# Two neighbouring scans of 1024 elements as one of 2048, with a zero factor where the second begins

## The reference

```python
x = x + 0.5 * ffn(layernorm(x), W1, b1, W2, b2)
x = x + ssm(layernorm(x), ...)
x = x + 0.5 * ffn(layernorm(x), W1, b1, W2, b2)
```

```python
u  = silu(conv4(x_in) + conv_b); dt = softplus(x_in[:, :32] @ Wdt.T + bdt); A = -exp(A_log)
h  = h * exp(dt * A) + dt * Bm * u      # for each channel and state, token by token, h = 0 first
y  = sum over states of h * Cm;  out = (y * silu(z)) @ Wo.T + bo + x * mean(Dv)
```

## Time and profile before

| | |
|---|---|
| runs shown | 768.38, 767.89, 770.54 us, median 768.38 |
| profiled execution | 768.11 us, span 766.3 us |
| VectorE busy | 669.7 us (87%) |
| TensorE busy | 640.7 us (84%), mean granted clock 0.919 |
| ScalarE busy | 603.2 us (79%) |
| GpSimd busy | 301.7 us (39%) |

### The profile page before, as it was taken

The page is one execution under the profiler, slowest core; times in us unless marked ns, Lnnn a source line. Parts: engine busy times, 40 slices in busy tenths (PEclk is TensorE's granted clock), DMA queues, the critical chain, the costliest instruction groups (busy, mean ns, idle before and its releaser), DMA issues. The chain is left out here.

```text
span 766.3 us, 8284 instructions
## 1 busy us (share of the span) xinstructions
PE 640.7 (84%) x2912; PEld 331.8 (43%) x2912; DVE 669.7 (87%) x463; ACT 603.2 (79%) x1066; POOL 301.7 (39%) x189
## 2 busy tenths in 40 slices
PE   7967786889886999979898999967867997874958
PEld 5642333364342466445244574622322654241727
DVE  2436948779999999999999999999999999999791
ACT  2478896779798989998788989898889787946454
POOL 0107020034344598569920767066940060600030
PEclk9997898989997899999999999996988999896979
DMA  8330476350838070421567150705161504205001
GB/s 299 139 137 28 160 219 184 125 178 28 313 117 313 1 246 2 172 103 60 215 198 269 50 198 13 262 1 219 28 216 59 216 31 176 99 28 219 2 0 56
DMA packets 40026, 103.08 MB, mean 135 GB/s; under 512 B 4080, under 2 KB 13040, under 8 KB 39984
## 3 DMA queue, kind: packets, MB, share of 16 engines
q1 hardware_dynamic: 37424, 94.40, 33.7%
q10 hardware_dynamic: 2560, 8.14, 4.5%
HBM read 23.08 MB, written 4.19 MB: 36 GB/s over the span
## 5 line engine op out<-in xcount | busy, mean ns | idle before, releaser
L1089 ACT ACTIVATE G<-RD,COL 128x1024 f32<-128x1024 f32 (+1 forms) x288 | 280.0, 1043 | 62.0 <-PE Y L1376 55.6
L1209 DVE TENSOR_TENSOR_SCAN G<-G,STT,RV 128x1024 f32<-128x1024 f32 (+1 forms) x160 | 312.5, 2015 | 6.4 <-ACT G L1089 6.4
L1209 DVE TENSOR_TENSOR_SCAN G<-G,RV 128x1024 f32<-128x1024 f32 (+1 forms) x128 | 268.9, 2157 | 13.4 <-ACT G L1089 13.4
L1376 PE MATMUL Y<-G,RW 128*32 128x512 f32 x1024 | 143.7, 678 | 62.2 <-DVE G L1209 58.9
L823 POOL TENSOR_SCALAR LV<-LV 128x4 f32<-128x4 f32 x19 | 16.2, 854 | 298.0 <-ACT XN L910 297.7
L1376 PEld LDWEIGHTS Y<-G,RW 128*32 128x32 f32 x1024 | 27.8, 116 | 143.2 <-DVE G L1209 81.5
L849 POOL TENSOR_SCALAR XN<-X,LV 128x256 f32<-128x256 f32 x38 | 83.9, 2212 | 2.0
L1343 PE MATMUL MB<-XI,DIAG 128*64 128x512 f32 x248 | 62.8, 644 | 13.0 <-DMA XI<-XI 11.1
L1302 PE MATMUL MB<-MT,XF 128*128 128x256 f32 x240 | 62.3, 406 | 13.3 <-ACT MT L952 7.6
L832 POOL TENSOR_TENSOR LV<-LV,HALF 128x4 f32<-128x4 f32 (+1 forms) x25 | 45.9, 1837 | 63.5 <-DVE LV L1164 61.9
L1321 PE MATMUL MB<-XT,WI 128*128 128x512 f32 x128 | 64.1, 629 | 3.7 <-ACT XT L936 3.7
(11 more groups left out here) (93 smaller groups left out, 774.5 us busy)
## 6 DMA issues: line engine op xcount, KB each, us to landing
RD<-DW SPq DMA_DIRECT2D x60, 512.0 KB, 3.8
RV<-DW SPq DMA_DIRECT2D x60, 512.0 KB, 4.7
W<-in_w SPq DMA_DIRECT2D x48, 256.5 KB, 3.7
XI<-XI ACTq DMA_DIRECT2D x30, 256.5 KB, 5.0
X<-in_x SPq DMA_DIRECT2D x8, 512.0 KB, 5.6
out<-X SPq DMA_DIRECT2D x7, 512.0 KB, 3.2
G<-in_w SPq DMA_DIRECT2D x4, 513.0 KB, 7.8
RV<-in_w SPq DMA_DIRECT2D x4, 513.0 KB, 12.3
```

The costliest lines, as they stand in the source:

```text
L1089: eng.activation(G[:, i % NG, t0:t1], RD[:, q, t0:t1], ACT.Exp, scale=NAC[:, states(i):states(i) + 1]).then_inc(sems["exp"])
L1209: eng.tensor_tensor_scan(g, g, RV[:, (4 * k + q) % NR, t0:t1], STT[:, idx:idx + 1] if goes_on else 0.0, ALU.mult, ALU.add).then_inc(sems[" ...
L1376: ins = eng.matmul(Y[32 * q:32 * q + 32, 512 * h:512 * h + 512], RW[:, states(i + o), :], G[:, (i + o) % NG, 512 * h:512 * h + 512], start ...
```

## The change

In blocks 1, 2, 3, 8, 9, 10 and 11 (`paired`), scan q even and scan q + 1 become one instruction over 2048 elements: their G tiles and their RV tiles are neighbours. So that the second half begins with state zero, its first factor is made zero: the first column of RD[:, 1] and RD[:, 3] holds 1e30, and exp(1e30 * NAC) is 0, with NAC at most -1e-20. The copies into RD[:, 1] and RD[:, 3] leave out the first column in parts 0 and 2 (1023 elements a row in place of 1024). ScalarE writes the column twice in the program: at the start, and after the exp of 7/15 since part 1 overwrites it. The instruction waits for the exp and the RV copy of both scans, and it raises the semaphore by 2.

```diff
+def paired(i):
+    k = UNITS[i][0]
+    return runs(k) == 1 and k // 4 % 2 == 0
...
+                if n == AT[7, 0, 15]:
+                    do("huge", 1)
...
+                    if k // 4 % 2 == 0 and q % 2 and t0 == 0:
+                        t0 = 1
                     eng.dma_start(RD[:, q, t0:t1], fourfold(DW[q:P:4, 0, t0:t1])
...
+                elif stage == "huge":
+                    n, = a
+                    e.wait_ge("half")
+                    if n:
+                        e.wait_ge("exp", AT[7, 0, 15])
+                    eng.activation(RD[:, 1:4:2, 0], START[:, :], ACT.Copy).then_inc(sems["huge"])
...
-                    eng.tensor_scalar(NAC, NAC, -1.0, None, ALU.mult).then_inc(sems["nac"])
+                    eng.tensor_scalar(NAC, NAC, -1.0, -LEAST, ALU.mult, ALU.min).then_inc(sems["nac"])
...
-                    g = G[:, i % NG, t0:t1]
-                    eng.tensor_tensor_scan(g, g, RV[:, (4 * k + q) % NR, t0:t1], STT[:, idx:idx + 1] if goes_on else 0.0,
-                                           ALU.mult, ALU.add).then_inc(sems["scan"])
+                    if paired(i):
+                        if q % 2 == 0:
+                            e.wait_ge("repw", k, q + 1, 0)
+                            e.wait_ge("exp", i + 1)
+                            g = G[:, i % NG:i % NG + 2, :].rearrange("p a n -> p (a n)")
+                            r = (4 * k + q) % NR
+                            eng.tensor_tensor_scan(g, g, RV[:, r:r + 2, :].rearrange("p a n -> p (a n)"), 0.0,
+                                                   ALU.mult, ALU.add).then_inc(sems["scan"], 2)
+                    else:
+                        ...
```

More of the change, by code:

```diff
@@ L14 @@
 EPS = 1e-5
+HUGE, LEAST = 1e30, 1e-20
 TOP = 17.0
@@ L513, in schedule @@
         do(stage)
+    do("huge", 0)
     a, b, c = norm(0), norm(1), norm(2)
@@ L660, in build @@
         ZERO = sb("ZERO", [P, 3])
+        START = sb("START", [P, 2])
         TOPC = sb("TOPC", [P, 4])
@@ L817, in do @@
                     eng.memset(ZERO[:, :], 0.0)
+                    eng.memset(START[:, :], HUGE)
                     eng.memset(HALF[:, :], -0.5).then_inc(sems["half"])
@@ L1081, in do @@
                     e.wait_ge("nac")
+                    e.wait_ge("huge", k // 8)
                     e.wait_ge("mm", 7)
@@ L1207, in do @@
                         e.wait_ge("save", AT[ko, po, 4 * m])
-                    g = G[:, i % NG, t0:t1]
-                    eng.tensor_tensor_scan(g, g, RV[:, (4 * k + q) % NR, t0:t1], STT[:, idx:idx + 1] if goes_on else 0.0,
-                                           ALU.mult, ALU.add).then_inc(sems["scan"])
+                    if paired(i):
[7 more added lines that the diff above has]
+                    else:
+                        g = G[:, i % NG, t0:t1]
+                        eng.tensor_tensor_scan(g, g, RV[:, (4 * k + q) % NR, t0:t1], STT[:, idx:idx + 1] if goes_on else 0.0,
+                                               ALU.mult, ALU.add).then_inc(sems["scan"])
                 elif stage == "yz":
```

## The result

The changed kernel takes 788.36 us (median of 4 runs, 784.05 to 789.04) where the kernel before takes 768.13 us in the runs beside it: a ratio of 1.025, 95% interval 1.0209 to 1.0291. It is slower, as forecast, but by 20 us and not by 3.7; the time lies outside the range.

What follows compares the result with a forecast made beforehand. VectorE's own work was taken to set the pace from 2/0 to the end of block 11. Up to 354.57 +3.8 us, mainly block 3's GpSimd delay, and blocks 8 to 11 -0.1: +3.7 on 768.11, 771.8 us; range 766.5 to 776.

Steps and rivals of the forecast that it cites:

- The saving of 0.05 us a pair: VectorE's scans: the fixed part per scan, taken from start to start, is saved once per pair; 56 pairs save 2.7 us.
- The estimates from the Trainium skill: Fixed cost of a VectorE instruction: by 58 cycles the pairs would save 3.4 us, by about 150 cycles 8.8 us.
- the wait for the second exp of 1.05 us at three places: At 2/0, 9/4 and 10/4 the pair starts 1.05 us later than the single scan, since it needs both exps.
- the copies of 1023 elements: Copies with rows starting 4 bytes off: between 3.8 and 5.0 us each, hidden at both ends, cost 0.
- dt of block 3: Moved later by the pairs, from 176.92 to near 180.0 us, still in time for TensorE's z matmuls; cost nothing.
- the [128 x 4] step under pairs: Small GpSimd step, 2.09 us under back to back single scans: near 4.2 us with pairs, as a sign of being right.
- the five terms given for blocks 8 to 11: VectorE's gains, second-exp delay and lost waits in blocks 8 to 11, said to make about -0.1 us in sum.
- msv [...] needs three ends: done at 218.3: Block 3: GpSimd's msv waits for three ends of pairs and is done at 218.3 us, against 211.6 before.
- rival 1: Block 3: msv needs two ends, mt at 214.0, TensorE's queue absorbs it; net -0.1 to +0.9, 768.0 to 769.0 us; chance 0.27.
- mt starts before 215 us: Block 3: a start of the transposes mt before 215 us was named as a sign that the forecast is wrong.
- In blocks 8 to 11 GpSimd's chains mostly meet dt, yz, w or norm tiles: Blocks 8 to 11: GpSimd gets in beside such work, no TensorE wait is sure to grow; sum -0.1 us.
- Rival 3: Longer GpSimd chains also hold back transposes or merge in blocks 8 to 11: another 3 to 4 us, 775 to 776; chance 0.10.

## Why the prediction was off

**Right.** The saving of 0.05 us a pair was right: the row at 498.01 of VectorE's timeline above, four pairs in 17.36 us, gives (17.36 - 4.44) / 3 = 4.31 us from start to start, against 2 x 2.18. The estimates from the Trainium skill (VectorE: DVE Perf Modes, The TRN2 errata) again agree at their lower end only. Also right were the wait for the second exp of 1.05 us at three places (1.07 to 1.11 us), the copies of 1023 elements (4.1 us against 3.8, and hidden), dt of block 3 (done at 180.4 us, forecast 180.0, and TensorE did not wait for it), and the [128 x 4] step under pairs (4.2 us forecast, 4.18 measured). The sign was right with its mechanism: GpSimd gets in where a scan ends, msv holds mt, mt holds the reduction, the reduction holds the exps. Two small sums were wrong: the five terms given for blocks 8 to 11 (+1.05, -0.8, +0.8, -0.4, -0.6) add up to +0.05 and not to -0.1, and from 9/4 to 12/0 the changed kernel gained 2.5 us, where these terms give 1.0.

**Block 3, near in size by luck, since two errors nearly cancel.** "msv [...] needs three ends: done at 218.3" was wrong. Each step took one pair's end (4.55 us), two ends in all, and mt began at 214.65 us. That was near rival 1's number, 214.0, and it was one of my own signs against the forecast ("mt starts before 215 us"). But rival 1 let TensorE's queue take the delay up, and it could not: after 4.24 us of idle time its reduction ran at 1.2 GHz, 3.64 us in place of 1.92. So pair 3/4 started at 221.69, between 223.5 and 219.1, 4/0 was 3.65 us late where the forecast had 5.2, and 7/0 3.15 where it had 3.8.

**The step that failed** is "In blocks 8 to 11 GpSimd's chains mostly meet dt, yz, w or norm tiles, in which GpSimd gets in, and I see no TensorE wait that is sure to grow; sum -0.1". The profile shows +14.7 us from 8/4 to 9/4 in place of about +1, and the pairs of block 8 alone cost 14.8 us of the median. I had laid out block 3 end by end, and for block 8 I looked at what stood beside the chain, not at how long it would be. The trace of before had all that was needed: chain and msv ended at 440.94 and mt ran at 443.60, 2.7 us later. Most of its eight steps wait for an end (six of them under pairs, all longer than 4 us now), so ends half as frequent had to cost far more than 2.7 us; they cost 12.9. The sum after the fact: the chain starts 6.75 us late with ScalarE's statistics and takes 12.9 us longer, 19.7; less the slack of 2.7, mt should be 17.0 us late, and it was 17.2 (460.78); the matmuls between mt and the reduction run in part at 1.2 GHz, +2.4; the exps of 9/0 are 19.6 us late, and pair 9/4 needs the second of its own four, +1.1: 20.8.

**Rival 3** had the place and the mechanism ("in block 8 above all the mt behind its msv") and a price of 3 to 4 us, with no working behind it. It was worth 14 to 15, and its chance of 0.10 and the range's upper end of 776 us came from that price. Worked out as above it would have been the forecast.

**Not foreseen**: that TensorE's clock falls after such waits (block 3 +1.7 us on one reduction, block 8 +2.4 us). Block 7's 3 us in the profiled execution is the clock too, but kernels without pairs have it as well. How it shares in the median of 20 us stays open: filling that gap brought some 6 us of the median in the changed kernel (ratio 1.0169 in place of 1.025), with intervals that just touch (1.0209 and 1.0216), and nothing in kernels without GpSimd's delay.

## What to carry to other kernels

A longer instruction on one engine is not only cheaper per element. Where another engine gets in only at its ends, as GpSimd did here, it is also a longer time in which that engine gets nothing done, and each small step in that engine's chain can take one such time, at times two. Before merging, take each chain on the other engine, count its instructions, multiply by the new spacing of ends, and compare with the slack to the one who waits for the chain's last step; the smallest slack decides, not the busy share (GpSimd was busy for 39% here). The cure is as local as the harm: 0.6 us of work moved for one group gave back 17 us, and joining two small instructions into one gave back 9.

## What the hardware showed

- A GpSimd instruction under back to back VectorE scans mostly takes until the end of a scan, and hardly more for twice the elements: msv with [128 x 256] took 4.55 us and with [128 x 512] 4.76 us under scans of 4.3 us, and a [128 x 256] step took 0.5 to 0.56 us beside short work. The Trainium skill (SBUF — State Buffer, Who interferes with whom) says that such an instruction waits for the other to finish; the trace agrees, and adds that the price is per instruction. It can be two ends: the first step of msv took 4.48 us under scans of 1024 (at 204.65 in the kernel before, the second 2.43), and a norm tile took 8.98 us under pairs.
- A scan of 2048 is 4.44 us as shown and 4.31 from start to start, so the part that is fixed is 0.05 us between neighbours.
- In the changed kernel TensorE ran at 1.2 GHz behind idle times of 3.62 and 4.24 us in blocks 7 and 3 (reductions of 3.52 and 3.64 us, 1.92 at 2.4 GHz) and of 10.46 us in block 8 (eight matmuls in 3.05 us, 1.89 at 2.4 GHz), and at 2.4 GHz behind one of 2.41 us (367.95); with zero matmuls in the same 3.6 us the clock stayed at 1.00. The last idle time alone does not tell the level: the kernel before had a reduction of 2.44 us behind 2.57 us (364.90), and with zero matmuls one of 3.33 us behind 2.40 us (362.38).
